# Attention block, 64 images of 14x14x768: output projection turned weight-stationary, and every step laid out anew in twelve slots

## What is computed

```python
xn  = groupnorm(x, 32 groups)                          # over H, W and the group's channels
qkv = xn @ qkv_w.T + qkv_b                             # low-rank terms are added to the q and v thirds
attn = (q * hd**-0.5) @ k.T + rel_h + rel_w            # rel_* = q against relative position tables
out = softmax(attn) @ v
y   = x + out @ proj_w.T + proj_b
```

## Time and profile before

| | us |
|---|---|
| median of 3 runs | 3608.06 |
| the profiled execution | 3603.43 |
| its span (first to last instruction) | 3601.9 |
| mean granted clock of TensorE, share of full | 0.985 |
| TensorE matmul busy | 3447.5 (96%) |
| VectorE busy | 2573.5 (71%) |
| ScalarE busy | 2019.3 (56%) |
| 16 DMA engines, mean of their busy share | about 50% |

### The profile page before, as it was taken

How to read it: one execution, slowest core, us unless ns; L and a number is a source line. 1 busy time by engine, 2 the same in 40 slices (tenths; PEclk the granted TensorE clock), 3 DMA queues, 4 the chain that set the end, 5 groups by cost and what they waited for, 6 DMA issues and landing times.

```text
span 3601.9 us, 81066 instructions
## 1 busy us (share of the span) xinstructions
PE 3447.5 (96%) x32612; PEld 2313.4 (64%) x32612; DVE 2573.5 (71%) x6042; ACT 2019.3 (56%) x5459; POOL 35.7 (1%) x65
## 2 busy tenths in 40 slices
PE   5789999999999999999999999999999999999997
PEld 3556666666666666666666666666666666666665
DVE  5677777777777777777777777777777777777764
ACT  1466555555555555555656555556555555655553
POOL 0000000000000000000000000000000000000000
PEclk9899999999999999999999999999999999999998
DMA  4145555555455545455555565555455554555444
GB/s 120 35 98 108 111 107 110 104 107 111 102 104 112 106 102 114 100 107 107 109 105 111 97 116 102 106 105 109 102 115 104 108 104 104 104 115 105 108 94 92
DMA packets 992579, 376.18 MB, mean 104 GB/s; under 512 B 922307, under 2 KB 972483, under 8 KB 992206
## 3 DMA queue, kind: packets, MB, share of 16 engines
q1 hardware_dynamic: 976366, 333.63, 47.3%
q10 hardware_dynamic: 15840, 37.38, 3.6%
HBM read 86.61 MB, written 38.54 MB: 35 GB/s over the span
## 4 chain that ended last, share of the span: by engine, by line
PE 75%; DVE 14%; ACT 5%; DMA 1%; issue 1%; SPq 1%; POOL 0%; POOLq 0%; DVEq 0%; ACTq 0%
PE ring L614 39%; PE ring L684 20%; PE score L657 7%; PE o_ps L671 5%; ACT prob L740 3%; DVE split L854 3%; PE ring L692 2%; PE ring L681 2%; DVE rel_sb L823 2%; DVE row_max L831 2%; DVE q_lo L798 1%; DVE xT L802 1%; DVE rel_sb L817 1%; DVE split L845 1%; DMA rel_q<-rel_sb 1%
## 5 line engine op out<-in xcount | busy, mean ns | idle before, releaser
L614 PE MATMUL ring<-xn_hi,w_hi 128*128 128x392 f16 x3456 | 1149.9, 333 | 62.4 <-DVE rel_sb L823 57.7
L614 PE MATMUL ring<-xn_hi,w_lo 128*128 128x392 f16 x3456 | 1147.5, 332 | 0.0
L614 PE MATMUL ring<-xn_lo,w_hi 128*128 128x392 f16 x3456 | 1147.5, 332 | 0.0
L740 ACT ACTIVATE prob<-score,neg_max,exp_scale 98x196 f32<-98x196 f32 x1536 | 770.3, 511 | 484.2 <-DVE neg_max L835 476.5
L854 DVE SCALAR_TENSOR_TENSOR split<-prob,row_inv,split 98x196 f16<-98x196 f32 x1536 | 544.6, 418 | 12.4
L614 PEld LDWEIGHTS ring<-xn_hi,w_hi 128*128 128x128 f16 x3456 | 340.4, 98 | 317.3 <-DVE rel_sb L823 64.8
L684 PE MATMUL ring<-w_hi,o_hi 128*98 128x384 f16 x1536 | 501.7, 327 | 0.0
L684 PE MATMUL ring<-w_hi,o_lo 128*98 128x384 f16 x1536 | 501.7, 327 | 0.0
L684 PE MATMUL ring<-w_lo,o_hi 128*98 128x384 f16 x1536 | 501.5, 327 | 0.0
L614 PEld LDWEIGHTS ring<-xn_hi,w_lo 128*128 128x128 f16 x3456 | 340.8, 99 | 240.7 <-issue 8.8
L614 PEld LDWEIGHTS ring<-xn_lo,w_hi 128*128 128x128 f16 x3456 | 341.0, 99 | 224.2 <-issue 8.6
(11 more groups left out here) (121 smaller groups left out, 4919.8 us busy)
## 6 DMA issues: line engine op xcount, KB each, us to landing
y_sb<-in_x SPq DMA_DIRECT2D x256, 147.0 KB
out<-y_sb SPq DMA_DIRECT2D x256, 147.0 KB
x_sb<-in_x ACTq DMA_DIRECT2D x31, 1176.0 KB
rel_q<-rel_sb SPq DMA_DIRECT2D x128, 147.0 KB, 3.0
stage<-in_L_conv_qkv_w SPq DMA_DIRECT2D x3, 2304.0 KB, 18.9
turned<-split SPq DMA_TRANSPOSE x384, 4.0
v_tok<-v_split SPq DMA_TRANSPOSE x192, 3.4
stage<-in_L_conv_proj_w SPq DMA_DIRECT2D x1, 2304.0 KB, 20.1
```

Source lines behind the costliest of these rows:

```text
L614: last = T.matmul(ring[:, bank, 0:NT], w[:, c, 128 * j:128 * j + 128], xx[:, t.par, c, :], start=(c == 0 and part == 0), stop=(c == CT - 1 ...
L740: last = A.activation(prob[:, step[3], head, half, :], score[0:HALF, head, TOK * half:TOK * half + TOK], ACT.Exp, bias=neg_max[:, step[3], ...
```

## The change

- Y has six steps in place of eight: 128 output channels of the weights are stationary, and all 392 tokens move, 18 matmuls of the form of Q, K and V. ScalarE writes the result with scale and bias into a fp32 tile `yT`. A new step Z turns it back: four fp32 TensorE transposes into one ring bank. VectorE adds x there, and SyncE loads and stores x and y in blocks of 98 x 4 x 128.
- The bias matmul, its tiles, and their making in the preparation are gone.
- All lists are laid out anew in twelve slots, one S to each, with P of unit u-2 behind S of unit u. X of a pair stands in two slots and starts two pairs ahead.
- The bank of a ring step is its running number over the whole program, modulo 5, so the user before is always the fifth step back.
- The relative copies are in two parts: CA (head pairs 0 to 4) after the fifth has been scored, and CB (the last head pair) after unit 11.
- `prob` has one buffer, not two, and `o_hi` and `o_lo` two full ones.

```diff
-MIDDLE = (
...
+PE_ORDER = (
+    each("S", 0, 0) + each("P", 1, 10) + each("Z", 2, 5) + each("X", -1, 3, 4, 5) + each("V", 0, 0)
+    + each("S", 0, 1) + each("P", 1, 11) + each("K", 0, 1) + each("Y", 1, 0) + each("G", -1, 0)
+    + each("S", 0, 2) + each("P", 0, 0) + each("G", -1, 1) + each("V", 0, 1) + each("Y", 1, 1) + each("Z", 1, 0)
+    + each("S", 0, 3) + each("P", 0, 1) + each("K", 0, 2) + each("Y", 1, 2) + each("Z", 1, 1)
+    + each("S", 0, 4) + each("P", 0, 2) + each("V", 0, 2) + each("Z", 1, 2) + each("Q", -1, 0)
+    + each("S", 0, 5) + each("P", 0, 3) + each("K", 0, 3) + each("Q", -1, 1)
+    + each("S", 0, 6) + each("P", 0, 4) + each("V", 0, 3) + each("Q", -1, 2, 3)
+    + each("S", 0, 7) + each("P", 0, 5) + each("K", 0, 4) + each("Q", -1, 4)
+    + each("S", 0, 8) + each("P", 0, 6) + each("Q", -1, 5) + each("V", 0, 4)
+    + each("S", 0, 9) + each("P", 0, 7) + each("R", -1, 0) + each("K", 0, 5) + each("R", -1, 1) + each("Y", 1, 3)
+    + each("S", 0, 10) + each("P", 0, 8) + each("R", -1, 2, 3, 4) + each("V", 0, 5) + each("Y", 1, 4) + each("Z", 1, 3)
+    + each("S", 0, 11) + each("P", 0, 9) + each("K", -1, 0) + each("X", -2, 0, 1, 2) + each("Y", 1, 5) + each("Z", 1, 4))
...
 ACT_ORDER = (
...
+    each("Y", 2, 5) + each("X", -1, 3) + each("N", 0, 0) + each("X", -1, 4, 5) + each("T", 0, 0)
+    + each("V", 0, 0) + each("P", 1, 11) + each("N", 0, 1) + each("K", 0, 1) + each("T", 0, 1)
...
+    + each("V", 0, 4) + each("P", 0, 7) + each("R", -1, 0) + soft(9) + each("K", 0, 5) + each("R", -1, 1)
+    + each("Y", 1, 3) + each("R", -1, 2) + each("N", 0, 10) + each("R", -1, 3, 4) + each("T", 0, 10) + each("V", 0, 5)
...
 DVE_ORDER = (
...
+    each("S", 0, 0) + each("Z", 2, 4) + each("X", -1, 3) + each("N", 0, 0) + each("T", 0, 0) + each("Z", 2, 5)
+    + each("X", -1, 4)
+    + each("V", 0, 0) + each("S", 0, 1) + each("P", 1, 11) + each("X", -1, 5) + each("M", -1, 0)
+    + each("N", 0, 1) + each("K", 0, 1) + each("T", 0, 1) + each("G", -1, 0)
+    + each("S", 0, 2) + each("G", -1, 1) + soft(2) + each("V", 0, 1) + each("H", -1, 0)
...
+    + each("S", 0, 9) + each("V", 0, 4) + each("P", 0, 7) + each("R", -1, 0) + soft(9) + each("K", 0, 5)
+    + each("R", -1, 1)
+    + each("S", 0, 10) + each("R", -1, 2) + each("N", 0, 10) + each("R", -1, 3, 4) + each("T", 0, 10) + each("V", 0, 5)
+    + each("S", 0, 11) + each("Z", 1, 3) + each("P", 0, 9) + each("N", 0, 11) + each("K", -1, 0) + each("T", 0, 11)
+    + each("X", -2, 0, 1, 2))
...
 SP_ORDER = (
...
+    each("ST", 2, 4) + each("CB", 0, 0) + each("T", 0, 0)
+    + each("VT", 0, 0) + each("LY", 1, 0) + each("ST", 2, 5) + each("T", 0, 1) + each("LY", 1, 1)
...
+    + each("CA", -1, 0) + each("T", 0, 10)
+    + each("VT", 0, 5) + each("ST", 1, 3) + each("T", 0, 11))
...
+    users = [step for step in sequence(PE_ORDER, pairs) if step[0] in PER_PAIR]
+    bank = {step: n % BANKS for n, step in enumerate(users)}
+    user_before = {step: users[n - BANKS] for n, step in enumerate(users) if n >= BANKS}
...
-                        T.matmul(to, ones[:, :], bias_rows[:, out_c], start=True, stop=False)
-                        for c in range(HP):
-                            for part, (w, oo) in enumerate(((w_hi, o_hi), (w_hi, o_lo), (w_lo, o_hi))):
-                                last = T.matmul(to, oo[:, o_slot(t.par, c), tok], w[:, c, 3 * C:][:, out_c],
-                                                start=False, stop=(c == HP - 1 and part == 2))
...
+                    for c in range(HP):
+                        for part, (w, oo) in enumerate(((w_hi, o_hi), (w_hi, o_lo), (w_lo, o_hi))):
+                            last = T.matmul(ring[:, bank, 0:NT], w[:, c, 128 * j:128 * j + 128], oo[:, par, c, :],
+                                            start=(c == 0 and part == 0), stop=(c == HP - 1 and part == 2))
...
+                elif kind == "Z":
+                    wait(pe, read["Y"], 6 * p + k + 1)
+                    for i in range(4):
+                        last = T.transpose(ring[0:HALF, bank, 128 * i:128 * i + 128],
+                                           yT[:, k % 2, HALF * i:HALF * i + HALF], ident[:, :])
...
+                    A.activation(yT[:, k % 2, :], ring[:, bank, 0:NT], ACT.Identity,
+                                 bias=bias[:, 3 * CT + k:3 * CT + k + 1],
+                                 scale=y_scale[:, :]).then_inc(read["Y"], 1)
...
+                    V.tensor_tensor(y_sb[:, k % YS], ring[0:HALF, bank, :].rearrange("p (a b) -> p a b", a=4),
+                                    y_sb[:, k % YS], ALU.add).then_inc(read["Z"], 1)
```

More of the change, by code:

```diff
@@ L138 @@
[L138 to L159, removed]
@@ L162 @@
[L162 to L183, removed]
@@ L553, in _, with copy_rel @@
         def _(sp):
-            def copy_rel(turn):
-                wait(sp, read["R"], RCH, turn.q, RCH)
+            def copy_rel(heads, copied):
                 for head in range(2):
@@ L595, in _ @@
+            for slot in range(YS):
                 sp.wait_ge(y_out[slot], 16 * 2 * pairs)
@@ new lines, in _ @@
+            for step in sequence(PE_ORDER, pairs):
+                kind, p, k = step
+                par = p % 2
+                if kind in PER_PAIR:
+                    bank = bank_of[step]
+                    if step in user_before:
+                        before, p_before, k_before = user_before[step]
+                        wait(pe, read[before], PER_PAIR[before] * p_before + k_before + 1)
+                if kind in ("Q", "K", "V"):
+                    j = CT * "QKV".index(kind) + k
+                    for c in range(CT):
+                        if kind == "Q" and k == 0 and c % 2 == 0:
+                            wait(pe, xn_lo_made, 3 * p + c // 2 + 1)
+                        for part, (w, xx) in enumerate(((w_hi, xn_hi), (w_hi, xn_lo), (w_lo, xn_hi))):
+                            last = T.matmul(ring[:, bank, 0:NT], w[:, c, 128 * j:128 * j + 128],
+                                            xx[:, par, c, :], start=(c == 0 and part == 0),
+                                            stop=(c == CT - 1 and part == 2))
+                    last.then_inc(done[kind], 1)
+                elif kind == "R":
+                    if k == 0:
+                        wait(pe, read["Q"], 6 * p + 6)
+                    T.matmul(ring[:, bank, 0:2], w_hi[:, 0, 0:128], w_hi[:, 0, 0:2], start=True, stop=True)
+                    n_rows = min(RC, H - RC * k)
+                    for i, row in enumerate(range(RC * k, RC * k + n_rows)):
+                        for part, (tab, qq, qw) in enumerate(((rt_hi, q_hi, qw_hi), (rt_hi, q_lo, qw_lo),
+                                                              (rt_lo, q_hi, qw_hi))):
+                            for ax in range(2):
@@ L772, in _ @@
         @block.gpsimd
         def _(pool):
-            def steps(phase, order, before, turn):
-                for step in order:
-                    if step[0] == "G" and step[2] == 1:
-                        t = turn.of(step[1])
-                        wait(pool, read["G"], 2, t.q, 2)
-                        G.tensor_tensor(rstd[:, :], var_eps[:, :], minus_half[:, :], ALU.pow).then_inc(rstd_made, 1)
             G.memset(split[:, :, :, :, :, :, :].rearrange("r s a b c d k -> r (s a b c d k)"), 0.0).then_inc(split_zeroed, 1)
```

717 lines of the change are left out of this document (318 added, 399 removed).

## The result

The changed kernel takes **3389.34 us** (median of 4 runs, 3388.14 to 3391.05); the kernel before, timed beside it, 3608.35. The ratio is 0.9399, 95% interval 0.9385 to 0.9413. The forecast was 3415 in a range of 3385 to 3500.

A forecast was written before the change was run, and what follows sets the result against it. TensorE was taken as the bound, busy 104.72 of a 106.57 us pair, plus one wait at V0. From 3603.4: -130 - 57 - 25 + 19 + 0 gives 3410; with the median 4.6 above, 3415 us, range 3385 to 3500.

The forecast's parts named there:

- TensorE's sum: Y and Z on TensorE: Y 7.05 us less per pair, Z 3.0 more, net 4.05 per pair, -130 us.
- Z's price: Z's 24 fp32 transposes per pair on TensorE: 0.125 us each, 0.5 per Z, 3.0 per pair.
- The wait and the clock: TensorE at V0: the 31 waits of 1.85 us go, -57 us, and the clock falls following them, -25 us.
- The walk: Slot-by-slot times of TensorE and VectorE in the new layout: G1 late by 0.6 us per pair, 0 to 2 possible.
- the new wait at G1: TensorE's G1 at 15.7 us after S0 waits for G0 at 16.3: 0.6 us per pair, +19 us.
- Edges: Preparation 5.5 us less, first pair +3, last pair's ends +2: together 0, with 12 either way.
- B: Slots 0 to 2: the wait moves there, 2.1 us per pair in place of 0.6, with clock falls; 3486 us, chance 0.20.
- C: Slots 11 and 0: transposes let the clock fall, 1.68 us per pair, 52 us in all; 3467 us, chance 0.06.
- D: Slots 9 and 10: VectorE's R chain becomes the bound, V5, X0 and X1 want banks; slower, 3615 us or more, chance 0.05.
- E: Z on TensorE costs 0.7 to 1.0 us, fp16/fp32 load switching not hidden: +38 to +96, about 3470 us; chance 0.07.
- the median: Whole kernel: the median of the runs lies 4.6 us above the profiled execution, taking 3410 to 3415 us.

The follow-up runs named there:

- the added operation: Changed kernel with one more VectorE operation per pair, a reduction of 768 weights just ahead of S of unit 1: 3413.45 us, ratio 0.9471.

## Why the prediction was right

**TensorE's sum.** 4.05 us less per pair was forecast; 104.72 to 100.47 is 4.25. By start times in the trace a Y step takes 2.99 now and 3.13 before, so Y takes 7.0 less per pair, as forecast. A Z takes 0.44 for its four transposes, and up to 0.09 more where the next step is a score; a Q, K or V step has the same 0.09 more there (3.08 for 2.99), so it is no price of going from fp32 to fp16 weights. The six Z are 3.0 together, as forecast. That makes 3.9; the rest is that the Q, K, V and X steps take 0.25 and 0.10 less in their new places, which the forecast had at nothing. The 128-column form costs what the Q, K, V rows said.

**Z's price** was taken between two rows of transposes, neither of them alike, and the lower one was misread: the 0.31 us of the earlier trace rows are three load records that overlap, and no pace of TensorE. The bounds given for it don't follow either: Z at 0.70 would leave 91 us, not 112. The run that doubled the transposes gives 0.109, under the 0.125 taken; that the six Z still come to the forecast 3.0 is luck, since the 0.09 ahead of a score makes up for it. X's 0.135 goes with its strided weights: a load of Z's contiguous weights is recorded with 0.13 us, one of X's strided ones with 0.24, and X, with fewer moving columns, is the slower. X's weights are also the wider, 128 columns to Z's 98. The preparation has both kinds at 128 columns, in one line of the kernel before:

```profile
L476 PEld LDWEIGHTS prep_ring<-ident,stage x144: 138/228/243, 70.9 to 104.0; 128*128 128x128 f32 x144
```

Its last 36 loads are the contiguous ones, recorded with 0.14 us each; the strided ones ahead of them take 0.21 to 0.24. So the stride, and not the width, makes the record long. That the loads set the pace of X was not tried by itself.

**The wait and the clock** went in full, 57 and 25 us as forecast, though of the 25 some 4 were short waits of S and not clock. The reason given was incomplete. The prediction put it as "By running numbers V0's bank was last used by Z4", as if the number did it. By the runs it is the lists: numbers alone gave 0.5%, and the old numbering in the new lists costs only 14 us. In the chain above both waits hang on VectorE's one piece of 8 us. In the new lists its R steps stand in slots 9 and 10 with a softmax between, and V0 and Y0 come a slot or more behind them; no run tells which of the two it takes. The walk priced the R steps rightly: it had VectorE end R1 10.6 us after slot 9 began, and the trace has the next operation at 1847.99 - 1837.38 = 10.6. Slot 9's first score, then VectorE:

```profile
1837.38 0.28 PE L584 MATMUL score<-k_hi,q_hi 64*98 64x196 f16 x2
```

```profile
1846.88 1.07 DVE L747 SCALAR_TENSOR_TENSOR rel_sb<-ring,rel_scale,rel_part 64x504 f16<-64x504 f32 x1
1847.99 0.97 DVE L754 TENSOR_REDUCE row_max<-score 98x4 f32<-98x784 f32 x1
```

**The step that failed in size** is the new wait at G1: 0.6 us per pair, +19 us, forecast; next to nothing measured. VectorE's and ScalarE's timeline, then TensorE's at G1, in the pair whose slot 0 starts at 1866.54:

```profile
1867.45 0.97 DVE L754 TENSOR_REDUCE row_max<-score 98x4 f32<-98x784 f32 x1 [1.02 <-PE score L584]
...
1869.55 0.51 ACT L667 ACTIVATE prob<-score,neg_max,exp_scale 98x196 f32<-98x196 f32 x1
...
1875.42 0.96 DVE L754 TENSOR_REDUCE row_max<-score 98x4 f32<-98x784 f32 x1
...
1876.55 0.62 DVE L783 SCALAR_TENSOR_TENSOR o_lo<-o_ps,bias,o_hi 128x392 f16<-128x392 f32 x1
...
1879.49 0.62 DVE L721 SCALAR_TENSOR_TENSOR k_lo<-ring,bias,k_hi 128x392 f16<-128x392 f32 x1
...
1881.93 0.16 DVE L809 TENSOR_TENSOR spread<-spread,mean_var 128x2 f32<-128x2 f32 x1
```

```profile
1882.24 0.35 PE L627 MATMUL ring<-spread,gmean 128*128 128x2 f32 x2
```

VectorE reached S1 8.88 us after the slot's start, where the walk said 9.45, and G0's result came at 1882.09, 15.55 us in, where it said 16.3. TensorE wanted G1 at 15.7, as walked. The walk was 0.75 us long on VectorE, and half of that is one term: X3 on ScalarE puts the exponentials of unit 0 off by 0.8 us, not 1.2. They start 1869.55 - 1867.45 = 2.10 us after the row maximum, where the earlier trace rows has 1.27. The rest is short records that overlap more than I allowed. The margin left is 0.1 us at G1, 0.4 at Y0 and 0.6 at S2, and the added operation shows that there is no more: this layout is full there, and not in slot 8, the only other place that was tried.

**Edges**: forecast 0 with 12 either way. Outside of the thirty pairs nothing is left over; in the prediction's own terms, which take off 31 waits, they cost about 3.

**The rivals.** B didn't come. Some wait at G1 stood only 0.1 us off, but B's of 2.1 us asked for a walk that is too short, and it was too long. C didn't: in the slots with the most transposes the clock stayed at 1.00, and twice as many in a piece left it at 1.00 in a pair. The Trainium skill, TensorE: Matmul & The Clock Gate, Part 4: PE-mode transpose, says they do not count as busy in the same way as a matmul; no run here shows a price for that among matmuls. D didn't: V5 and X have no idle time before them in a pair. E didn't: Z cost its expected value. The forecast was 26 us high: 19 from G1's wait, 6 from TensorE's sum and 3 from the median, which lies 1.2 and not 4.6 above the profiled execution, less the 3 at the edges.

**What stays open.** It wasn't tried which part of the new lists matters (R in two pieces, V0 and Y0 later, X in two slots, P before the ring steps), nor whether the fall of the clock follows the length of the wait or its moment; it came behind 12 of 30 waits of 1.85 us before, every third of the 2.17 us ones with three operations added, and all from the twelfth pair on in the run with Y's form alone.

## What to carry to other kernels

A shorter step on the bound engine pays only as far as the lists leave the others room: in the old lists the cheaper projection, without turning back and with two neighbouring steps emptied, gave 78 us of its 211, and banks and projection together 131, where the full change gave 219 with 2.3 us more work per pair. Find the engine's longest piece without a partner (here VectorE's K0 and four R) before renumbering buffers: here a new number alone mostly moved its wait. Where margins are read off a trace, test them with one added operation there and one elsewhere.

## What the runs showed of the hardware

- fp32 transposes on TensorE of 128 moving columns run 0.109 us apart when the weights lie contiguous, and those with 98 columns 0.133 apart when the weights' elements lie 6 apart; the load records are 0.13 and 0.24 us. Of weights 128 columns wide the preparation has contiguous loads of 0.14 us and strided ones of 0.21 to 0.24.
- Waits of 2.4 and 1.8 us in each pair, by turns 40 and 62 us apart, had no clock fall behind them from the second to the eleventh pair (granted clock 1.00) and then had one behind each, for the rest of the loop (0.97), in the run with Y's form alone.
